# Rotary turn on the raw projections, squares on ScalarE: a fused layer of four blocks on one core

## The reference

```python
x = x + attn_a(layernorm(x))        # feature map elu+1, running sums over 16 heads
x = x + ffn(layernorm(x))           # relu(x @ Wq1.T + b1) @ Wq2.T + b2, weights in {-1, 0, 1}
x = x + attn_b(layernorm(x))
x = x + ffn(layernorm(x))

def attn_b(x):                      # 16 query heads, 4 key and value heads, head width 16
    q, k, v = x @ Wq.T, x @ Wk.T, x @ Wv.T
    q, k = rms_norm(q), rms_norm(k)             # v * rsqrt(mean(v * v) + 1e-6), per head
    q, k = rotary(q, cos, sin), rotary(k, cos, sin)   # (v1 cos + v2 sin, -v1 sin + v2 cos)
    q = q * q_gain
    att = softmax(mask_window_64(q @ k.T / 4))
    return pair_mix(att @ v) @ Wo.T
```

## Time and profile before

| what | value |
|---|---|
| time, median of 3 runs | 3313.47 us (3312.93 to 3314.41) |
| time of the profiled execution | 3308.83 us |
| its span in the trace | 3306.9 us |
| TensorE busy | 3088.1 us, 93% |
| VectorE busy | 2398.5 us, 73% |
| ScalarE busy | 1788.9 us, 54% |
| GpSimd busy | 545.9 us, 17% |
| mean granted clock of TensorE | 0.969 |

### The profile page before, as it was taken

One profiled execution on the slowest core, in us unless ns is written; L12 is line 12 of the kernel. 1 busy time (PEld: TensorE's weight loads), 2 busy tenths in 40 slices (PEclk: granted clock), 3 DMA queues, 4 the chain that ended last, 5 costly groups with the idle time before them and its releaser, 6 DMA issues.

```text
span 3306.9 us, 79649 instructions
## 1 busy us (share of the span) xinstructions
PE 3088.1 (93%) x27330; PEld 2456.8 (74%) x27330; DVE 2398.5 (73%) x5990; ACT 1788.9 (54%) x3585; POOL 545.9 (17%) x1164
## 2 busy tenths in 40 slices
PE   3789999999999999999999999999999999999977
PEld 2567777777777777777777777777777777777755
DVE  4567777777777777777777777777777777777754
ACT  1255555565555565555565555566554556555554
POOL 0012111112111112111112111112111111111111
PEclk9899999999999999999999999999999999999998
DMA  1000000000000000000000000000000000000000
GB/s 60 8 10 16 15 2 15 13 15 15 15 2 15 13 15 15 15 2 15 13 15 15 15 8 9 13 15 15 15 15 2 13 15 15 15 15 2 14 10 16
DMA packets 42084, 44.86 MB, mean 14 GB/s; under 512 B 2608, under 2 KB 41392, under 8 KB 42032
## 3 DMA queue, kind: packets, MB, share of 16 engines
q1 hardware_dynamic: 42032, 44.20, 4.4%
HBM read 21.12 MB, written 16.78 MB: 11 GB/s over the span
## 4 chain that ended last, share of the span: by engine, by line
PE 77%; issue 8%; DVE 6%; ACT 4%; POOL 4%; DMA 0%; POOLq 0%; SPq 0%; DVEq 0%; ACTq 0%
PE Q L364 14%; PE HID L414 13%; PE Y L435 13%; PE Q L555 8%; PE HID L372 4%; PE Q L823 4%; PE Q L593 3%; PE Q L588 3%; PE Q L757 2%; PE Q L606 2%; PE Q L837 2%; PE Q L733 1%; ACT a_qz L1123 1%; PE Q L762 1%; PE Q L570 1%
## 5 line engine op out<-in xcount | busy, mean ns | idle before, releaser
L435 PE MATMUL Y<-w2t,f_hh 128*128 128x256 f32 x2048 | 550.9, 302 | 72.5 <-DVE f_hl L1307 72.3
L949 ACT ACTIVATE f_r<-HID,b1c 128x512 f32<-128x512 f32 x512 | 350.9, 685 | 327.8 <-PE HID L414 240.9
L435 PE MATMUL Y<-w2t,f_hl 128*128 128x256 f32 x2048 | 519.5, 286 | 0.0
L435 PEld LDWEIGHTS Y<-w2t,f_hh 128*128 128x128 f32 x2048 | 395.0, 193 | 141.8 <-DVE f_hl L1307 83.8
L1307 DVE TENSOR_TENSOR f_hl<-f_r,f_hh 128x512 fp32r<-128x512 f32 x512 | 351.6, 687 | 188.1 <-ACT f_hh L950 185.8
L414 PE MATMUL HID<-ff_xh,w1t 128*128 128x512 f32 x1024 | 448.9, 438 | 14.8 <-DVE ff_xl L1299 14.8
L414 PE MATMUL HID<-ff_xl,w1t 128*128 128x512 f32 x1024 | 419.5, 410 | 0.0
L435 PEld LDWEIGHTS Y<-w2t,f_hl 128*128 128x128 f32 x2048 | 397.1, 194 | 4.2
L1409 DVE TENSOR_TENSOR a_s<-Q,cst 128x512 f32<-128x512 f32 x512 | 329.3, 685 | 76.6 <-PE Q L555 68.9
L950 ACT ACTIVATE f_hh<-HID,b1c 128x512 fp32r<-128x512 f32 x512 | 351.9, 687 | 0.0
L1123 ACT ACTIVATE a_qz<-Q 128x512 f32<-128x512 f32 x512 | 279.1, 602 | 46.8 <-PE Q L762 46.5
(11 more groups left out here) (186 smaller groups left out, 7048.4 us busy)
## 6 DMA issues: line engine op xcount, KB each, us to landing
...
```

The costliest lines, as they stand in the source:

```text
L435: mm = pe.matmul(Y[t // 2][:, (t % 2) * D:(t % 2 + 1) * D], h[:, fb % 2, t * P:(t + 1) * P], w2t[:, fb, :], start=False, stop=(fb == FB - ...
L949: act.activation(f_r[:, fb % 2, :], HID[fb % 2][:], ACT.Relu, bias=b1c[:, fb:fb + 1]).then_inc(f_rr, 1)
```

## The change

In block B the rotary turn comes first and the norm behind it: cosines and sines take b_raw, rotate makes their sum in b_qn, and norm_qk multiplies that by b_rs into b_qr, from which the stacks are made. (The inverse root and the gain are one factor per head, so the two can be swapped.) The squares move from GpSimd to ScalarE, as the first of three instructions of `raw`, out of the same PSUM bank as the copy. GpSimd keeps sines and norm_rstd. And the lists of calls of all four engines are written in another order, in both phases.

```diff
                 act.wait_ge(b_qkv, b * NT + t + 1)
+                if needed(b * NT + t - 1):
+                    act.wait_ge(b_ss_s, b * NT + t - 1)
+                act.activation(b_sq[:, t % 2], Q[t % 2][:, 0:QK], ACT.Square).then_inc(b_sq_s, 1)
                 act.activation(b_raw[:, t], Q[t % 2][:, 0:QK], ACT.Copy).then_inc(b_raw_s, 1)
...
                     def cosines(t):
                         j = b * NT + t
-                        dve.wait_ge(b_qn_s, j + 1)
+                        dve.wait_ge(b_raw_s, j + 1)
                         if needed(j - 1):
-                            dve.wait_ge(b_lo, j - 1)
-                        dve.tensor_tensor(b_qr[:, t % 2], b_qn[:, t % 2], table("cos", t, 0, HD), ALU.mult).then_inc(b_rc_s, 1)
+                            dve.wait_ge(b_qr_s, j - 1)
+                        dve.tensor_tensor(b_qn[:, t % 2], b_raw[:, t].rearrange("p (h j) -> p h j", j=HD), table("cos", t, 0, HD),
+                                          ALU.mult).then_inc(b_rc_s, 1)
...
-                        dve.tensor_tensor(b_qr[:, t % 2], b_qr[:, t % 2], b_rsn[:, t % 2], ALU.add).then_inc(b_qr_s, 1)
+                        dve.tensor_tensor(b_qn[:, t % 2], b_qn[:, t % 2], b_rsn[:, t % 2], ALU.add).then_inc(b_rot, 1)
+
+                    def norm_qk(t):
+                        j = b * NT + t
+                        dve.wait_ge(b_rs_s, b * 2 + min(t, 1) + 1)
+                        dve.wait_ge(b_rot, j + 1)
+                        if needed(j - 1):
+                            dve.wait_ge(b_lo, j - 1)
+                        dve.tensor_tensor(b_qr[:, t % 2], b_qn[:, t % 2],
+                                          b_rs[:, t, :].unsqueeze(2).broadcast_to([P, H + KVH, HD]), ALU.mult).then_inc(b_qr_s, 1)
...
                     def sines(t):
                         j = b * NT + t
-                        pool.wait_ge(b_qn_s, j + 1)
+                        pool.wait_ge(b_raw_s, j + 1)
                         if needed(j - 1):
-                            pool.wait_ge(b_qr_s, j - 1)
+                            pool.wait_ge(b_rot, j - 1)
...
-                    def squares(t):
...
-                        pool.tensor_tensor(b_sq[:, t % 2], b_raw[:, t], b_raw[:, t], ALU.mult).then_inc(b_sq_s, 1)
```

255 lines of the change are left out of this document (124 added, 131 removed).

## The result

| | before | after |
|---|---|---|
| median of the runs that were compared | 3313.2 us | 3213.43 us (3209.77 to 3227.4, 4 runs) |
| ratio, 95% interval | | 0.9707 [0.9677, 0.9737] |
| span of the profiled execution | 3306.9 us | 3213.6 us |
| mean granted clock | 0.969 | 0.988 |

A forecast was written before the change was run, and what follows sets the result against it. TensorE, busy 93%, was taken as the bound, with down(5)'s 2.14 us wait each step. 2.1 - 0.6 = 1.5 us over 30 boundaries gives 45 us: 3308.83 to 3264, plus 4.6 is 3269, rounded to 3270; range 3255 to 3285.

The forecast's parts named there:

- The rest of both halves: Reordered lists outside the project(3) to turn_qk(1,0) stretch: small-slack places lose 0.6 us a step, bounds nought and 1.5.
- The passage: From project(3) to turn_qk(1,0), across the boundary between a step's halves: gain 2.1 us a step on average.
- the places that I had named: turn_y(0) behind normalise(0), next_norm(0) behind relu(2), turn_qk(3,0) behind evacuate(2,2): slack nought to 0.3 us each.
- one meeting with GpSimd: VectorE up to low(5): one instruction slowed beside GpSimd's sines, 0.45 us, moving low(5)'s end from +9.4 to +9.8.
- The clock stayed up: Granted clock near 1.00 through the boundary between halves, instead of about half behind down(5)'s stall.
- The number of steps: 30 steady boundaries at 1.5 us each make 45 us.
- the ends: First and last steps of the run: filled with other waits, nothing counted for them.
- (A): Clock still falls at the boundary between halves: 0.8 us a step lost, time 3294; chance 0.22.
- (B): ScalarE becomes the bound at the end of the first half, b_v(0) delaying qkv(2) by 0.46: time 3334; chance 0.14.
- (C): Same time: all three VectorE meetings with GpSimd paid, small waits come to 1.2 us: 3313; chance 0.09.
- (D): More comes back: no meeting, no small waits, 2.45 us a step, time 3240; chance 0.05.

The follow-up runs named there:

- after_old_first_half: Changed kernel with the first half's lists of TensorE, ScalarE and VectorE back in the order of before; 3219.23 us, ratio 0.9712.
- before_new_first_half: Kernel before with the changed order of the first half on TensorE, ScalarE and VectorE, second half and GpSimd as before; 3315.19 us, ratio 1.0003.
- neighbours_bad: Changed kernel with one exchange in TensorE's first-half list, down(7) ahead of state(1); 3236.48 us, ratio 0.9765.
- after_old_second_tail: Changed kernel with the old second-half lists behind scores(3) on TensorE, exps(3) on ScalarE and cosines(2) on VectorE; 3221.38 us, ratio 0.9722.
- ops_up7: Kernel before with turn first, squares on ScalarE and old lists, except up(7) ahead of down(5) and turn_qk(0,0); 3258.63 us, ratio 0.9836.
- after_rstd_first: Changed kernel with GpSimd's norm_rstd of the feed-forward back ahead of sines(0) and sines(1); 3349.59 us, ratio 1.0116.

## Why the prediction was wrong in size

**The rest of both halves** is the step that failed: I took a loss of 0.6 a step, with bounds of nought and 1.5. It is a gain of 0.83 (0.10, 0.28 and 0.46 in the three stretches behind the passage), and my bounds left no room for a gain. Moving the lists shows that it is the lists' own: 0.45 for the first half, 0.2 to 0.3 for the tail of the second. I had looked at places where slack might vanish and never at those where slack was already missing, since no bracket stood there. The kernel before had such a place, in the earlier trace rows' step: up(4), whose last matmul starts at 1658.35, and turn_y(3).

```profile
1658.35 0.40 PE L414 MATMUL HID<-ff_xl,w1t 128*128 128x512 f32 x1
...
1658.82 0.44 PE L612 MATMUL Q<-cst,a_y 128*128 128x128 f32 x2
```

From start to start are 0.47, and turn_y(3) starts as VectorE ends a_y (1658.34 + 0.42). In after the same two are 0.22 apart:

```profile
1618.77 0.39 PE L414 MATMUL HID<-ff_xl,w1t 128*128 128x512 f32 x1
1618.99 0.38 PE L612 MATMUL Q<-cst,a_y 128*128 128x128 f32 x2
```

So 0.25 of the 0.46 is a wait that went, and it goes with the lists: the same two take 0.48 in after_old_first_half and 0.23 in before_new_first_half. The first half has three more places where the same pair of neighbours takes unlike times (medians over the steps, from start to start). own_norm to state(0) takes 0.20 before and 0.11 after. The second matmul behind each of these two waits comes another 0.06 and 0.07 later. Against that, one of the places that I had named did cost: in after next_norm(0) behind scores(2,1) stands 0.10 longer than next_norm(1) behind scores(3,1), 1.16 and 1.06. The fourth, down(2) to project(3), costs after 0.02. Together the waits account for 0.35 of the 0.46; about 0.1 is left for what stands beside what.

That last part was argued and not shown. By starts in after, the last matmul of a turn (L606, L612) or a state (L570) takes 0.03 when up or down follow, 0.11 when next_norm does, and 0.20 when scores or numer do, whose matmuls use 32 or 64 of the 128 rows or columns; behind up or down the difference is 0.09. The Trainium skill, "TensorEngine Tiling (Array Packing)", section "Key Properties", says that a change of the tiling mode drains TensorE; the difference fits it. But the one exchange that was made for it, neighbours_bad, gave 0.01 where 0.09 was expected. The 0.10 and 0.28 of the two other stretches go with the lists of the second half (after_old_second_tail gives 0.19 of the 0.28); what in them does it stays open.

**The passage** was taken as 2.1 and measured 2.43; it was the smaller error. By its steps:
- qkv(2) starts at +2.21, not +2.32, and waits 0.35 from start to start, not 0.46 (its bracket of 0.18 is too short): relu(4) ended at +1.39, as said, but the square began 0.11 ahead of that, at +1.28, since neighbours on ScalarE overlap; the three instructions took 0.87 as forecast (0.88).
- VectorE's second half starts at +2.93 (forecast +3.05), low(5) ends at +9.34. I had +9.8 with one meeting with GpSimd ahead of it. There was one, in low(5) itself (0.31); cosines(0), rotate(0) and norm_qk(0) cost 0.09 together. The rule from "SBUF — State Buffer" in the Trainium skill is that the two contend; that VectorE pays each time, which made it +10.75, was my reading. The trace has the contention, but GpSimd's sines(1) were the ones that waited there (0.75 and 0.84).
- down(5): +9.39 against +9.8, and 0.3 of wait against 0.7, because VectorE was 0.46 earlier; turn_qk(0,0) +10.90 (+11.2), waits from start to start 0.45, 0.35 and about 0.55 (0.45, 0.35, 0.6); scores(0) +12.96 (+13.3); turn_qk(1,0) +16.80 (+17.2). Each number behind down(5) carries the same 0.3 to 0.4, so the sizes behind it were right.
- The clock stayed up in the traced run, as taken.
- A wait was not named at all: ScalarE's squares wait for VectorE's sums. In after it hurts nobody (1.05, with relu(5) in time), but on the old lists it held up low(5) by 0.59 and up(7) by 0.36.

**The number of steps** and the ends were right within 5 us. The sum: (2.43 - 2.1) + (0.83 + 0.6) = 1.76 a step, by 30 makes 53; the miss is 57. The traced run of before lay 4.6 below its median, which the forecast had added, and that of after 2.2 above its own; with 1.5 of rounding, less the 4.5 at the ends, this makes the other 4.

The rivals. (A), the clock, did not come, but was nearer than its 0.22 says: ops_up7, with waits of 0.2 to 0.8 and none longer, lost the clock 12 times, and neighbours_bad, whose passage has the waits of after, 4 times. (B), ScalarE: its place was right (b_v), its price 0.35. (C) rested on meetings and small waits that did not come. (D) took 2.45 for the passage, which is what it gave (2.43), though with one meeting; it missed the rest of both halves.

What was right: the order on GpSimd decides (after_rstd_first, 4.3 a step), and its squares made part of the stall. Moving them alone takes it from 2.14 to 1.35 and 1.28 of the 3.26; the rest of the stall needed up(7) and VectorE's order together.
